# Moving VectorE's row statistics of the feed-forward norm behind the next softmax maxima, in a gated recurrence beside a six-layer local-attention transformer on one core

## Chip, cores and metric

The kernel runs on one core of a Trainium2 chip. The metric is the device time of one execution in microseconds (us), taken from several executions; lower is better. Beside it stands one execution taken with the hardware profiler, whose trace gives the start and length of every instruction on each engine: TensorE (PE), VectorE (DVE), ScalarE (ACT), GpSimd (POOL) and the queue of SyncE (SP), which issues the DMAs.

## The reference, cut to what matters

The input is 2 streams of 1024 tokens of 128 features, in float32. Its normalised form goes through a gated linear recurrence (s) and, independently, through six transformer layers (g); the output is x + s * silu(g).

```python
def attn_layer(x, Wqkv, qs, ksc, Wo):
    q, k, v = jnp.split(x @ Wqkv, 3, -1)          # 16 heads of 64
    q = l2norm(q) * qs; k = l2norm(k) * ksc        # then rotary tables with a decay
    out = local_attention(q, k, v)                 # windows of 32, looking back one window
    return out @ Wo

def ffn_layer(x, g, bln, W1, b1, W2, b2):
    mu = x.mean(-1, keepdims=True)
    var = ((x - mu) ** 2).mean(-1, keepdims=True)
    xn = (x - mu) / jnp.sqrt(var + 1e-05) * g + bln
    a, gate = jnp.split(xn @ W1 + b1, 2, -1)
    return a * jax.nn.gelu(gate, approximate=False) @ W2 + b2

for i in range(DEPTH):                             # DEPTH = 6
    x = attn_layer(shift_tokens(x), ...) + x
    x = ffn_layer(shift_tokens(x), ...) + x
```

## The kernel before

The tokens are cut into 8 tiles of 128, so that six layers make 48 steps. A step i works on one tile of both streams, b = 0 and b = 1, in two half steps, and it is a software pipeline: while the projections of step i run, the keys and queries of step i - 1 are transposed and scored, the softmax and the values of step i - 2 are done, and the feed-forward norm of step i - 3 and the feed-forward of step i - 4 go with the first half step. A step inside its layer is called by its tile, t = 0 to 7. In the last steps (from step 40) the recurrence's work is added.

Every engine has its own instruction stream, written out by hand as a function half(i, b), and the engines wait for each other by semaphores alone. What stands in one half step of an engine is carried out in exactly the written order; a wait holds all that is behind it. There is no scheduler.

What the change and the prediction touch:

- **VectorE.** maxima (line 1561 of the profile, rmax<-ps_s) reads the scores in PSUM when TensorE has filled them (scores_filled). less_max (L1569) subtracts the maxima. rotate (L1535 and L1538, two instructions for each of four chunks of 512 columns) waits for ScalarE's square of the chunk and frees its PSUM bank for TensorE. square_sums is L1548, the gate products of the feed-forward are L1661. mid_variance is the step that moves: two row statistics (L1598), two aggregates (L1601), the negated mean (L1616) and the variance with its epsilon (L1617, ss<-mid_mv), whose semaphore is mid_var.
- **GpSimd.** floor(i, 0) (L1986, floored<-ss) takes the 32 square sums of stream 0 together with the 2 variances of the norm in one instruction of 34 columns, so it waits for both. Behind it stand the Newton step (L1994 to L2000), the scaling of stream 0's keys and queries (L2028), the adds of the rotary halves (L2016), the scaling of probabilities (L2038, pr), the low parts of the projection input (L2051), and then floor(i, 1) for stream 1.
- **ScalarE.** inverse_root (L1208 logarithm, L1212 exponential) waits for the floor. Behind it on ScalarE stand the square of the first chunk (L1166) and the copies of transposed probabilities (L1154, pbd<-ps_tr, two instructions for each of two banks). In half step (i, 1) the first pair of copies stands ahead of the root; in half step (i + 1, 0) both pairs stand behind it, except at a layer's first tile.
- **TensorE.** The transposes of the probabilities (L803) and of the keys (first eight L816 of a half step) share two PSUM banks: the fifth key transpose writes the bank that the second pair of copies (L1154) empties.

Of the kernel before, what the change touches and what calls it, by code (L numbers as in the profile page):

```python
# [91 lines left out]
def valid(step):  # L92

    return not step.fixed or 0 <= step.n < STEPS
# [52 lines left out]
def next_tile(i, b):  # L147
    return (i + 1, 0) if b else (i, 1)
# [215 lines left out]
def layers(nc, a, x, xmid, branch, ident, eps_col, w, rec):  # L364

    with ExitStack() as ctx:
# [152 lines left out]
        def wait_fill(eng, sems, order, i, what):  # L519
            if exists(order, i, what):  # L520
                bank, n = fill(order, i, what)
                eng.wait_ge(sems[bank], n)
# [5 lines left out]
        def softmax_tile(i, b):  # L528
            return (i - 1, 0) if b else (i - 2, 1)
# [21 lines left out]
        with nc.Block() as block:  # L551
# [965 lines left out]
            def _(dve):  # L1517
                v = nc.vector

                def rotate(i, b, c):  # L1520
                    if not valid(i):
                        return
                    k, part = c // 2, slice(c * COLS, (c + 1) * COLS)
                    bank, n = fill(qn_order, i, ("qkv", b, c))
                    if c % 2 == 0:
                        if b:
                            dve.wait_ge(added[0], 2 * i.n + k + 1)
                        elif not i.first:
                            dve.wait_ge(added[1], 2 * i.n + k - 1)
                    if c == 0:  # L1530
                        dve.wait_ge(tab_ready, i.n + 1)
                        after_first(dve, qk_ready[b], 2 * i.n, i)
                    dve.wait_ge(squared[b], 4 * i.n + c + 1)
                    swapped = ps_qn[bank][:, :].rearrange("p (h s d) -> p h s d", s=2, d=DH // 2)[:, :, ::-1, :]
                    v.tensor_tensor(t2[:, part].rearrange("p (h s d) -> p h s d", s=2, d=DH // 2), swapped,  # L1535
                                    tab[:, 2 * k + 1:2 * k + 2, :].rearrange("p o (s d) -> p o s d", s=2)
                                    .broadcast_to([P, HEADS // 2, 2, DH // 2]), ALU.mult)
                    v.tensor_tensor(qk[b][:, part].rearrange("p (h d) -> p h d", d=DH),  # L1538
                                    ps_qn[bank][:, :].rearrange("p (h d) -> p h d", d=DH),
                                    tab[:, 2 * k:2 * k + 1, :].broadcast_to([P, HEADS // 2, DH]),  # L1540
                                    ALU.mult).then_inc(qn_done[bank], 1)
# [15 lines left out]
                def maxima(j, b):  # L1557
                    if not valid(j):
                        return
                    dve.wait_ge(s_full, 2 * j.n + b + 1)  # L1560
                    v.tensor_reduce(rmax[b][:, :], ps_s[:, :, :, :].rearrange("p h m k -> p (h m) k"), AX.X,  # L1561
                                    ALU.max).then_inc(max_ready[b], 1)

                def less_max(j, b):
                    if not valid(j):
                        return
                    dve.wait_ge(max_ready[b], j.n + 1)
                    wait_fill(dve, tr_full, tr_order, j + 1, ("probs", b, 1))
                    v.tensor_tensor(pr[b][:, :, :, :].rearrange("p m h k -> p h m k"), ps_s[:, :, :, :],  # L1569
                                    rmax[b][:, :].rearrange("p (h m) -> p h m", h=2).unsqueeze(3).broadcast_to([P, 2, HP, 2 * WINDOW]),  # L1570
                                    ALU.subtract).then_inc(s_read, 1)
# [21 lines left out]
                def mid_statistics(n):  # L1593

                    dve.wait_ge(fx_in, (n.n + 1) * SHIFT_DMAS)
                    after_first(dve, normed, n.n, n)
                    for s in range(B):
                        v.bn_stats(mid_stats[:, s, :], mid(n, s, MIXED)).then_inc(mid_stat, 1)  # L1598
                    dve.wait_ge(mid_stat, 2 * B * n.n + B)
                    for s in range(B):  # L1600
                        v.bn_aggr(mid_mv[:, s, :], mid_stats[:, s, :]).then_inc(mid_stat, 1)  # L1601
                    dve.wait_ge(mid_stat, 2 * B * (n.n + 1))
# [6 lines left out]
                def mid_variance(i):  # L1609
                    n = i - 3  # L1610
                    if not valid(n):
                        return
                    mid_statistics(n)
                    if not n.first:
                        dve.wait_ge(newton[0], NEWTON * i.n)
                    v.tensor_scalar(minus_mean[:, :], mid_mv[:, :, 0], -1.0, None, ALU.mult)  # L1616
                    v.tensor_scalar(ss[0][:, 2 * HEADS:], mid_mv[:, :, 1], LN_EPS, None, ALU.add).then_inc(mid_var, 1)  # L1617

                def take_out(i, b):
                    if not exists(pv_order, i, ("out", b)):  # L1620
                        return
                    j, m = i - 2 - b, i - 4
                    bank = taken(i, ("out", b))
                    if valid(j):
                        last = residual(bank, j, b)
                    if b == 0 and i.n < STEPS and valid(m):
                        last = update_x(bank, m)
                    last.then_inc(pv_done[bank], 1)
# [100 lines left out]
                def input_stats(columns, part):  # L1729
                    for c in columns:  # L1730
                        dve.wait_ge(x_in[part], 32)
                        v.bn_stats(stats[:, c, :], in_tile(c)).then_inc(s_st, 1)
# [81 lines left out]
                def half(i, b):  # L1814
                    soft = softmax_tile(i, b)
                    maxima(*soft)
                    less_max(*soft)
                    for c in range(4):
                        rotate(i, b, c)
                        if b == 0 and c == 0:  # L1820
                            take_out(i, 1)
                        if (i.n, b, c) == (0, 0, 1):
                            input_stats(range(HEAD, 8), 1)
                        if (i.n, b, c) == (0, 1, 1):
                            input_moments(range(HEAD, COLUMNS), HEAD + COLUMNS)
                        if (i.n, b, c) == (1, 1, 1):
                            copy_pair(0)
                        if c == 1:
                            if b == 1:
                                if i.t == TILES - 1 and not i.last_layer:  # L1830
                                    high_q(i.layer + 1)
                                take_out(i, 0)
                            row_sums(*soft)
                            row_recips(*soft)
                    if b == 0:
                        rec_driving(i - 1, 1)
                    if i.first and b == 0:
                        low_x(i, 1)
                        copy_head(B, HEAD)
                    if (i.n, b) == (1, 1):  # L1840
                        copy_pair(1)
                    if (i.n, b) == (3, 1):
                        softplus_recip()
                    if (i.n, b) == (0, 1):
                        low_x(*next_tile(i, b))
                    rec_conv1d(i, b)
                    recurrent = b == 0 and rec_tile(i, b, RATES_AT) is not None
                    if b == 0 and not recurrent:
                        ffn_gate(i, 0)
                    square_sums(i, b)  # L1850
                    rec_admission(i, b)
                    rec_scan(i, b)
                    if recurrent:
                        ffn_gate(i, 0)
                    if (i.n, b) == (1, 0):
                        low_x(*next_tile(i, b))
                    if b == 0:
                        ffn_gate(i, 1)
                        ffn_gate(i, 2)
                        mid_variance(i)  # L1860
                    elif i.t == 3:
                        low_w1(i.layer)
                    if (i.n, b) == (0, 0):
                        input_stats(range(8, COLUMNS), 1)
                    if (i.n, b) == (0, 1):
                        tables(i + 1)
                        input_root(1)
                    if (i.n, b) == (1, 1):
                        copy_pair(2)
# [407 lines left out]
```

## Time and profile before

| | |
|---|---|
| time, median of 3 runs | 1550.27 us (1549.19 to 1552.37) |
| time of the profiled execution | 1548.62 us |
| its span from first to last instruction | 1546.8 us |
| granted TensorE clock, mean | 0.995 |
| TensorE busy | 1499.9 us, 97% of the span |
| ScalarE busy | 1346.7 us, 87% |
| GpSimd busy | 1291.4 us, 83% |
| VectorE busy | 1283.4 us, 83% |

A busy share is a mean over the span. The profile's times are of one execution; a wait is idle time of the engine ahead of an instruction, with what ended it behind the arrow.

### The profile page before, as it was taken

What the parts mean: (1) busy time and instruction counts of PE and PEld (TensorE: products, weight loads), DVE (VectorE), ACT (ScalarE), POOL (GpSimd) and SP (SyncE); (2) the same over time, 40 slices, a digit from 0 to 9 for tenths busy, and PEclk for the clock granted to TensorE, in tenths of its full rate; (3) what the DMA queues carried; (4) which work ended last, traced back from release to release, by engine and by line L of the source; (5) the groups of instructions that cost most, each with busy time, mean ns of one, the idle gap of its engine ahead of it and who ended that gap; (6) DMA issues with size and microseconds to landing.
All of it is one profiled execution on the core that took longest, in us unless ns stands there. A gap on an engine that the chain in (4) does not pass through costs nothing.

```text
span 1546.8 us, 64269 instructions
## 1 busy us (share of the span) xinstructions
PE 1499.9 (97%) x26170; PEld 1306.7 (84%) x26170; DVE 1283.4 (83%) x2033; ACT 1346.7 (87%) x2600; POOL 1291.4 (83%) x1268
## 2 busy tenths in 40 slices
PE   6899999999999999999999999999999999999996
PEld 3688888888888888888888888888888888888885
DVE  7888888888889878788878878887888878888876
ACT  5779998999998889898989999889899889989974
POOL 8899899978889888899888899888989977767741
PEclk8999999999999999999999999999999999999999
DMA  5344433454343444434354433444433333333232
GB/s 142 88 111 118 100 83 89 103 128 109 87 103 73 101 118 123 96 86 102 74 128 117 102 90 88 101 101 124 108 89 89 86 76 96 91 80 74 65 91 57
DMA packets 219395, 150.44 MB, mean 97 GB/s; under 512 B 144604, under 2 KB 166752, under 8 KB 219104
## 3 DMA queue, kind: packets, MB, share of 16 engines
q1 hardware_dynamic: 219104, 146.33, 39.2%
q8 instruction: 211, 3.46, 1.0%
q14 instruction: 80, 0.66, 0.1%
HBM read 27.50 MB, written 1.05 MB: 18 GB/s over the span
## 4 chain that ended last, share of the span: by engine, by line
PE 81%; issue 5%; POOL 5%; DVE 4%; ACT 4%; SPq 1%; DMA 0%; POOLq 0%; ACTq 0%; DVEq 0%
PE ps_pv L877 11%; PE ps_tr L816 10%; PE ps_pv L909 9%; PE ps_qn L791 8%; PE ps_s L856 8%; PE ps_qn L793 7%; PE ps_qn L792 7%; PE ps_tr L803 5%; PE ps_pv L889 3%; PE ps_s L838 2%; PE ps_pv L927 2%; POOL qk L2016 2%; PE ps_pv L929 2%; PE ps_pv L928 2%; POOL qkr L2028 1%
## 5 line engine op out<-in xcount | busy, mean ns | idle before, releaser
L2016 POOL TENSOR_TENSOR qk<-qk,t 128x1024 f32<-128x1024 f32 x192 | 459.8, 2395 | 1.6 <-ACT v_new L1249 1.1
L2028 POOL TENSOR_TENSOR qkr<-qk,rinv 128x1024 f32<-128x1024 f32 x192 | 363.9, 1907 | 3.7 <-POOL rinv L2000 0.2
L1535 DVE TENSOR_TENSOR t<-ps_qn,tab 128x512 f32<-128x512 f32 x384 | 260.8, 679 | 87.3 <-ACT sq L1166 79.0
L791 PE MATMUL ps_qn<-w_hi,xs_hi 128*128 128x512 f32 x576 | 252.8, 439 | 16.0 <-DVE qk L1538 12.1
L1538 DVE TENSOR_TENSOR qk<-ps_qn,tab 128x512 f32<-128x512 f32 x384 | 261.2, 680 | 0.0
L1166 ACT ACTIVATE sq<-ps_qn 128x512 f32<-128x512 f32 x384 | 229.6, 599 | 27.7 <-PE ps_qn L793 17.9
L1154 ACT ACTIVATE pbd<-ps_tr 64x512 f32<-64x512 f32 x384 | 225.7, 588 | 12.2 <-PE ps_tr L803 8.8
L793 PE MATMUL ps_qn<-w_hi,xs_lo 128*128 128x512 f32 x576 | 229.1, 398 | 0.0
L792 PE MATMUL ps_qn<-w_lo,xs_hi 128*128 128x512 f32 x576 | 228.9, 397 | 0.0
L1548 DVE TENSOR_REDUCE ss<-sq 128x32 f32<-128x2048 f32 x96 | 218.4, 2275 | 0.0
L816 PE MATMUL ps_tr<-ident,qkr 128*128 128x128 f32 x1536 | 210.6, 274 | 5.8 <-ACT pbd L1154 2.5
L877 PEld LDWEIGHTS ps_pv<-pbd,v_win 128*64 128x64 f32 x6144 | 187.5, 138 | 25.2 <-issue 24.7
L816 PEld LDWEIGHTS ps_tr<-ident,qkr 128*128 128x128 f32 x1536 | 175.2, 141 | 34.0 <-issue 18.2
L877 PE MATMUL ps_pv<-pbd,v_win 128*64 128x64 f32 x6144 | 200.9, 224 | 0.0
L2038 POOL TENSOR_TENSOR pr<-pr,rrec 128x1024 f32<-128x1024 f32 x96 | 183.4, 1911 | 16.3 <-issue 11.1
L909 PE MATMUL ps_pv<-wo,oT 128*128 128x128 f32 x1536 | 187.2, 275 | 1.4 <-DVE oT L1555 1.4
L909 PEld LDWEIGHTS ps_pv<-wo,oT 128*128 128x128 f32 x1536 | 182.6, 192 | 6.0 <-DVE oT L1555 1.2
L1561 DVE TENSOR_REDUCE rmax<-ps_s 128x16 f32<-128x1024 f32 x96 | 117.1, 1220 | 67.0 <-PE ps_s L856 64.4
L856 PE MATMUL ps_s<-kT,qT 64*32 64x64 f32 x12288 | 151.7, 225 | 5.2 <-issue 4.8
L856 PEld LDWEIGHTS ps_s<-kT,qT 64*32 64x32 f32 x12288 | 135.1, 105 | 23.5 <-issue 22.3
L791 PEld LDWEIGHTS ps_qn<-w_hi,xs_hi 128*128 128x128 f32 x576 | 109.4, 190 | 46.7 <-issue 16.8
L1986 POOL TENSOR_SCALAR floored<-ss 128x34 f32<-128x34 f32 (+1 forms) x96 | 30.1, 313 | 121.3 <-DVE ss L1617 108.2
(178 smaller groups left out, 3024.8 us busy)
## 6 DMA issues: line engine op xcount, KB each, us to landing
v_win<-v_new SPq DMA_DIRECT2D x576, 128.0 KB
v_win<-v_new SPq DMA_DIRECT2D x192, 64.0 KB
v_win<-v_win SPq DMA_DIRECT2D x188, 64.0 KB, 2.0
kT<-kT SPq DMA_DIRECT2D x84, 128.0 KB, 2.7
w_raw<-in_Wqkv SPq DMA_DIRECT2D x18, 512.0 KB, 3.9
rot<-in_rot SPq DMA_DIRECT2D x48, 128.0 KB, 3.5
wo<-in_Wo SPq DMA_DIRECT2D x6, 512.0 KB, 4.7
x<-x SPq DMA_DIRECT2D x48, 56.0 KB
```

The costliest lines, as they stand in the source:

```text
L791: mm(ps_qn[bank][:, :], xs_hi[b][:, :], w_hi[:, part], start=True, stop=False)
L792: mm(ps_qn[bank][:, :], xs_hi[b][:, :], w_lo[:, part], start=False, stop=False)
L793: mm(ps_qn[bank][:, :], xs_lo[b][:, :], w_hi[:, part], start=False, stop=True).then_inc(qn_full[bank], 1)
L816: last = tr(ps_tr[bank][:, m * P:(m + 1) * P], qkr[b][:, (4 * f + m) * P:(4 * f + m + 1) * P], ident[:, :])
L856: last = mm(ps_s[q, h, hp, :], qT[rows, hp, q], kT[b][rows, hp, WINDOW * w:WINDOW * (w + 2)], start=False, stop=hp == HP - 1)
L877: last = mm(pv_target(bank, hp, w), v_win[b][:, w, hp * DH:(hp + 1) * DH], pbd[:, hp, :, WINDOW * w:WINDOW * (w + 1)], start=True, stop=True)
L909: last = mm(ps_pv[bank][:, 0:P], oT[:, n // 2, n % 2, :], wo[:, n, :], start=(n == 0), stop=(n == HP - 1))
L1166: f(sq[:, c * COLS:(c + 1) * COLS], ps_qn[bank][:, :], ACT.Square).then_inc(squared[b], 1)
L1535: v.tensor_tensor(t2[:, part].rearrange("p (h s d) -> p h s d", s=2, d=DH // 2), swapped, tab[:, 2 * k + 1:2 * k + 2, :].rearrange("p o (s ...
L1538: v.tensor_tensor(qk[b][:, part].rearrange("p (h d) -> p h d", d=DH), ps_qn[bank][:, :].rearrange("p (h d) -> p h d", d=DH), tab[:, 2 * k: ...
L2016: g.tensor_tensor(qk[b][:, part], qk[b][:, part], t2[:, part], ALU.add).then_inc(added[b], 1)
L2028: g.tensor_tensor(qkr[b][:, part].rearrange("p (h d) -> p h d", d=DH), qk[b][:, part].rearrange("p (h d) -> p h d", d=DH), rinv[b][:, k * ...
```

## The change

mid_variance is taken from the end of VectorE's half step (i, 0) and put into half step (i, 1), between maxima and less_max. Nothing else is edited; the instructions and their number stay the same on all engines.

```diff
@@ -1814,6 +1814,8 @@
                 def half(i, b):
                     soft = softmax_tile(i, b)
                     maxima(*soft)
+                    if b == 1:
+                        mid_variance(i)
                     less_max(*soft)
                     for c in range(4):
                         rotate(i, b, c)
@@ -1857,7 +1859,6 @@
                     if b == 0:
                         ffn_gate(i, 1)
                         ffn_gate(i, 2)
-                        mid_variance(i)
                     elif i.t == 3:
                         low_w1(i.layer)
```

VectorE's stream before, around the border between half step (4, 0) and half step (4, 1); the names in square brackets are the semaphores that an instruction waits for:

```order
L1661 SCALAR_TENSOR_TENSOR hid<-ps_pv,b,hid 128x256 [waits gelu_ready]
L1661 SCALAR_TENSOR_TENSOR hid<-ps_pv,b,hid 85x256 [waits gelu_ready]
L1598 BN_STATS mid_stats<-xmid 128x6 [waits mid_normalised,mid_shifted]
L1598 BN_STATS mid_stats<-xmid 128x6
L1601 BN_AGGR mid_mv<-mid_stats 128x2 [waits mid_stats_done]
L1601 BN_AGGR mid_mv<-mid_stats 128x2
L1616 TENSOR_SCALAR minus_mean<-mid_mv 128x2 [waits newton0,mid_stats_done]
L1617 TENSOR_SCALAR ss<-mid_mv 128x2
L1561 TENSOR_REDUCE rmax<-ps_s 128x16 [waits scores_filled]
L1569 TENSOR_TENSOR pr<-ps_s,rmax 128x2x8x64 [waits tr_filled0,max_ready0]
L1535 TENSOR_TENSOR t<-ps_qn,tab 128x512 [waits qk_ready1,squared1,tab_ready,added0]
```

The same place of the changed kernel:

```order
L1661 SCALAR_TENSOR_TENSOR hid<-ps_pv,b,hid 128x256 [waits gelu_ready]
L1661 SCALAR_TENSOR_TENSOR hid<-ps_pv,b,hid 85x256 [waits gelu_ready]
L1561 TENSOR_REDUCE rmax<-ps_s 128x16 [waits scores_filled]
L1598 BN_STATS mid_stats<-xmid 128x6 [waits mid_normalised,mid_shifted]
L1598 BN_STATS mid_stats<-xmid 128x6
L1601 BN_AGGR mid_mv<-mid_stats 128x2 [waits mid_stats_done]
L1601 BN_AGGR mid_mv<-mid_stats 128x2
L1616 TENSOR_SCALAR minus_mean<-mid_mv 128x2 [waits newton0,mid_stats_done]
L1617 TENSOR_SCALAR ss<-mid_mv 128x2
L1569 TENSOR_TENSOR pr<-ps_s,rmax 128x2x8x64 [waits tr_filled0,max_ready0]
L1535 TENSOR_TENSOR t<-ps_qn,tab 128x512 [waits qk_ready1,squared1,tab_ready,added0]
```

The reduction rmax<-ps_s, with its wait for scores_filled, moved ahead of the six instructions of mid_variance; the subtraction behind them stayed where it was. This is so in all 45 steps that have a mid_variance in half().

GpSimd's stream is the same in both kernels. This is what stands behind the wait for mid_var_done there, in half step (i, 1) of a step inside a layer:

```order
L1986 TENSOR_SCALAR floored<-ss 128x34 [waits mid_var_done,ss_sum0]
L1994 TENSOR_TENSOR newt<-rinv 128x34 [waits rooted0]
L1996 TENSOR_TENSOR newt<-newt,floored 128x34 [waits newton0]
L1998 TENSOR_SCALAR newt<-newt 128x34 [waits newton0]
L2000 TENSOR_TENSOR rinv<-rinv,newt 128x34 [waits newton0]
L2008 TENSOR_TENSOR mid_offset<-minus_mean,rinv 128x2 [waits mid_normalised,newton0]
L2028 TENSOR_TENSOR qkr<-qk,rinv 128x1024 [waits tr_filled1,tr_filled0,added0,newton0]
L2028 TENSOR_TENSOR qkr<-qk,rinv 128x1024 [waits tr_filled1,tr_filled0,added0]
L2016 TENSOR_TENSOR qk<-qk,t 128x1024 [waits qn_evacuated1,qn_evacuated0]
L2038 TENSOR_TENSOR pr<-pr,rrec 128x1024 [waits rec_ready0]
L2051 TENSOR_TENSOR xs_lo<-xsh,xs_hi 128x128 [waits tr_evacuated0]
L2016 TENSOR_TENSOR qk<-qk,t 128x1024 [waits qn_evacuated1,qn_evacuated0]
```

Nothing moved here. The next row of this stream is floor(i, 1), which feeds ScalarE's root of stream 1.

## Rows read from the trace of the kernel before

**Rows 1.** The page: the chain that ended last, by engine.
```profile
PE 81%; issue 5%; POOL 5%; DVE 4%; ACT 4%; SPq 1%; DMA 0%; POOLq 0%; ACTq 0%; DVEq 0%
```

**Rows 2.** Busy times in one inner step: PE, PEld, DVE, ACT, POOL, then clock and DMA.
```profile
851.78:881.68 29.90, 29.84 (x540) 26.34 (x539) 24.61 (x40) 26.88 (x52) 25.55 (x25) 1.00 0.44 110
```

**Rows 3.** The waits: engine and line, what it waited for, total us, times, longest.
```profile
POOL floored L1986 <- DVE ss L1617: 108.2, 45, 5.4
```

**Rows 4.** Timeline of VectorE, that step: start us, length us, instruction.
```profile
852.10 0.47 DVE L1598 BATCH_NORM_STATS2 mid_stats<-xmid 128x6 f32<-128x128 f32 x2
...
852.97 0.16 DVE L1617 TENSOR_SCALAR ss<-mid_mv 128x2 f32<-128x2 f32 x1
853.04 1.22 DVE L1561 TENSOR_REDUCE rmax<-ps_s 128x16 f32<-128x1024 f32 x1
854.29 1.23 DVE L1569 TENSOR_TENSOR pr<-ps_s,rmax 128x1024 f32<-128x1024 f32 x1
855.43 0.68 DVE L1535 TENSOR_TENSOR t<-ps_qn,tab 128x512 f32<-128x512 f32 x1
```

**Rows 5.** Timeline of GpSimd, that step.
```profile
853.29 0.29 POOL L1986 TENSOR_SCALAR floored<-ss 128x34 f32<-128x34 f32 x1 [2.10 <-DVE ss L1617]
...
866.70 0.29 POOL L1986 TENSOR_SCALAR floored<-ss 128x32 f32<-128x32 f32 x1
...
883.23 0.29 POOL L1986 TENSOR_SCALAR floored<-ss 128x34 f32<-128x34 f32 x1 [2.84 <-DVE ss L1617]
```

**Rows 6.** Timeline of ScalarE, that step.
```profile
853.80 0.23 ACT L1208 ACTIVATE log_ss<-floored 128x34 f32<-128x34 f32 x1
...
854.33 0.60 ACT L1166 ACTIVATE sq<-ps_qn 128x512 f32<-128x512 f32 x1
...
867.02 0.23 ACT L1208 ACTIVATE log_ss<-floored 128x32 f32<-128x32 f32 x1 [0.66 <-POOL floored L1986]
...
869.12 1.19 ACT L1154 ACTIVATE pbd<-ps_tr 64x512 f32<-64x512 f32 x2
```

**Rows 7.** Timeline of TensorE, that step.
```profile
850.77 1.01 PE L856 MATMUL ps_s<-kT,qT 64*32 64x64 f32 x69
...
858.73 0.40 PE L791 MATMUL ps_qn<-w_hi,xs_hi 128*128 128x512 f32 x1
...
870.62 1.04 PE L816 MATMUL ps_tr<-ident,qkr 128*128 128x128 f32 x8
```

**Rows 8.** Timeline of ScalarE, then TensorE, in step 41.
```profile
1269.46 1.18 ACT L1154 ACTIVATE pbd<-ps_tr 64x512 f32<-64x512 f32 x2
...
1270.79 0.63 PE L816 MATMUL ps_tr<-ident,qkr 128*128 128x128 f32 x4 [0.15 <-ACT pbd L1154]
```

**Rows 9.** Timeline of ScalarE, then TensorE: first and last of 26 steps.
```profile
175.99 1.18 ACT L1154 ACTIVATE pbd<-ps_tr 64x512 f32<-64x512 f32 x2
...
177.31 1.04 PE L816 MATMUL ps_tr<-ident,qkr 128*128 128x128 f32 x8
...
1170.73 1.18 ACT L1154 ACTIVATE pbd<-ps_tr 64x512 f32<-64x512 f32 x2
...
1172.25 1.04 PE L816 MATMUL ps_tr<-ident,qkr 128*128 128x128 f32 x8
```

**Rows 10.** Timeline of GpSimd, then TensorE, at a layer's first tile.
```profile
729.48 1.93 POOL L2038 TENSOR_TENSOR pr<-pr,rrec 128x1024 f32<-128x1024 f32 x1
...
731.76 2.40 POOL L2016 TENSOR_TENSOR qk<-qk,t 128x1024 f32<-128x1024 f32 x1
...
731.46 1.09 PE L803 MATMUL ps_tr<-ident,pr 128*128 128x128 f32 x8 [0.39 <-POOL pr L2038]
```

**Rows 11.** VectorE's negated mean: at that tile, then the group of all 45.
```profile
732.24 1.95 DVE L1616 TENSOR_SCALAR minus_mean<-mid_mv 128x2 f32<-128x2 f32 x1
...
L1616 DVE TENSOR_SCALAR minus_mean<-mid_mv 128x2 f32<-128x2 f32 x45 | 16.3, 363 | 1.5
```

**Rows 12.** Timeline of GpSimd in step 41, one of the recurrence's steps.
```profile
1266.81 0.53 POOL L1986 TENSOR_SCALAR floored<-ss 128x32 f32<-128x32 f32 x1 [1.73 <-DVE ss L1548]
```

## The prediction

> **What bounds the kernel now.** I first read the chain that ended last: TensorE carries 81% of it, and no other engine more than 5% [rows 1]. Then one inner step by its busy times: TensorE is busy 29.84 of 29.90 us at full clock, ScalarE 26.88, GpSimd 25.55, VectorE 24.61 [rows 2]. So inside a layer a step takes as long as TensorE's own work. A delay elsewhere costs time only where it makes TensorE wait, and work saved elsewhere gives nothing. The question is how much slack lies between the moved instructions and TensorE.
>
> Third, the waits. The longest in the kernel is GpSimd's floor waiting for the last instruction of mid_variance: 108.2 us over 45 steps, 2.4 us each [rows 3]. GpSimd has nothing else to do then, so the step that moves is the one that another engine is standing still for. The wait itself costs nothing on TensorE's chain, but it says that whatever delays mid_variance delays everything behind the floor on GpSimd, at once and in full.
>
> Fourth, the timelines of that step. mid_variance starts at 852.10 and ends at 853.13; maxima follow without a gap at 853.04 and take 1.22 us, then less_max at 854.29, then the first rotate at 855.43 [rows 4]. TensorE's scores, which maxima wait for, were complete at 851.78 [rows 7], 0.3 us before mid_variance started. Maxima could therefore have run at 852.10.
>
> **What the change does in such a step.** No instruction is added; the order of two blocks is swapped.
>
> Maxima start at 852.10 instead of 853.04. mid_variance starts behind them at about 853.24 (consecutive VectorE instructions overlap by 0.08) and ends near 854.26, which is 1.13 us later. less_max comes at about the same time as before (it saves the 0.04 us gap ahead of it and gains an overlap, together 0.1 us), so ScalarE's exponentials gain nothing of use.
>
> The floor goes from 853.29 to 854.42, plus 1.13. ScalarE's logarithm started at 853.80, 0.22 us after the end of the floor at 853.58 [rows 5, 6]: ScalarE was still copying. Where it has to wait, it starts 0.03 us behind a floor (867.02 behind 866.99 [rows 5, 6]). So 0.18 us are absorbed and ScalarE's root is 0.95 us late. Queued behind it on ScalarE: the square of the first chunk, the second pair of probability copies, the next square, the exponentials, the key copies. Queued behind its result on GpSimd: Newton, both scalings, add, scaling of probabilities, low_x, add, floor(i, 1).
>
> *First rotate.* Its square ended at 854.93 and will end at 855.88 [rows 6], so rotate starts near 856.0 instead of 855.43. Two chunks later, at about 858.5, it frees the bank that TensorE fills at 858.73 [rows 7]. It just fits: zero, and up to 0.1 us if I am off.
>
> *GpSimd.* From floor(i, 0) to floor(i, 1) pass 13.41 us of work without an idle gap, apart from the wait for the root; floor(i, 1) has no wait of its own in this step [rows 5]. So floor(i, 1) is 0.95 us late too, ending at 867.94 instead of 866.99. ScalarE had already been idle for 0.66 us for it [rows 6], so nothing is absorbed: logarithm, copies, square and copies all come 0.95 late, and the second pair of copies, which ended at 870.31, ends at 871.26.
>
> *TensorE.* The fifth key transpose needs that pair's bank. Eight transposes take 1.04 us and four 0.63, so it starts 0.41 behind 870.62 [rows 7, 8], at 871.03: 0.7 us behind the copies. The least such distance, where TensorE really waits, is 0.15 [rows 8]. Free slack is about 0.57 us and the delay 0.95, so TensorE stalls for 0.38 us. The stall recurs each step, because TensorE, and with it the next scores and the next mid_variance, moves by only 0.38 while GpSimd's lateness begins anew. GpSimd's next floor waited 2.84 us [rows 5], so the delay does not pile up.
>
> I read the same distance in the 26 steps with t = 1 to 6 (steps 5 and 6, and six of each of four layers). The first gives 0.55 us and the last 0.75 by the same rows [rows 9]; the mean is 0.71, the least 0.50, the largest 1.04. Less 0.15, that is 0.56 of slack: **26 x 0.39 = 10 us**.
>
> *Steps 3 and 4.* There the distance was already at its least, 0.14. Their delay, 0.85 and 0.95 us, is paid in full: **1.8 us**.
>
> *Layer borders* (five, from t = 7 to the next layer's t = 0). GpSimd also splits the next layer's weights there and is idle nowhere between the t = 7 floor and the probabilities that TensorE waits for: they end at 731.41, and the transposes start at 731.46 after 0.39 us of idle time [rows 10]. A root that is 0.95 late at t = 7 comes out there whole in four borders, and 0.73 in one where 0.27 us lay between: **4.5 us**.
>
> *The floor at t = 0* doesn't move. There the negated mean took 1.95 us instead of the usual 0.17, and ended (734.19) when GpSimd's add did, at 734.16 [rows 10, 11]. Over the 45 steps this group holds 16.3 us where 45 x 0.17 = 7.7 would do, so 8.7 us of such holding [rows 11]. Moved 1.1 us later it is held until the same moment, so GpSimd's floor comes when it came; but maxima are then done before the hold, and rotate can start up to 0.56 us earlier. GpSimd still limits the next copies, so I give this back **-0.7 us** over the layer starts. Here the Trainium skill has a rule (SBUF — State Buffer, "SBUF: two separate sides"): VectorE and GpSimd share a port pair that is locked for a whole instruction, and the loser blocks completely. By that rule the hold ends with the add, as the trace shows.
>
> *Steps 41 to 47.* The scores come late there, and mid_variance is 2 us later, but floor(i, 1) waits 1.73 us for VectorE's square sums anyway [rows 12]. What is left is a bank or two at 0.1 us: **0.7 us**.
>
> Sum: 10 + 1.8 + 4.5 - 0.7 + 0.7 = 16.3 us. On the profiled execution's 1548.6 us that is 1565; the median of the runs is 1.7 us above it, so I predict **1566 us**, 1.1% slower.
>
> *Bounds of the unknown.* The trace has no floor at the new place. Two numbers carry the sum. The lateness of the root: at most the whole 1.13 us (nothing absorbed), which adds 0.18 to about 33 places, +6 us; at least 0.75, if maxima and the statistics overlap more than neighbours do now, -6 us. The slack: if TensorE can go on at 0.05 behind a release, as in [rows 10], instead of 0.15, -3 us. I stay with 0.95 and 0.15, since rows of the very same instructions show them. A gain on the sum would need TensorE's few waits to vanish, and the change shortens those only at layer starts.
>
> **Rivals.**
>
> *Hidden* (0.09). The 0.95 us are absorbed before TensorE. For it: mid_variance has 2.4 us of GpSimd idle time around it. Against: that idle time lies ahead of the floor, where it protects the next step and not this one, and the distances above are single readings. It needs the root to be less than about 0.55 us late. Result 1549 to 1553.
>
> *Faster* (0.07). The 8.7 us of holding shrink by 1.1 us in each of five places, maxima and less_max come earlier at t = 0, and TensorE's waits for rotate's banks there (0.3 to 0.6 us each) go. Worth up to 2 or 3 us if the root's lateness is free; it decides only from there. Against: TensorE's layer starts are limited by GpSimd. By the port rule of the Trainium skill, named above, a later negated mean is held for less, which is this case. Result about 1547.
>
> *Nothing absorbed* (0.14). The lateness passes to TensorE whole, 0.95 us in each of 38 steps, because rotate's bank and the copies miss one after the other: 36 us, 1586.
>
> *Queue position.* That ScalarE's late key and value copies cost TensorE a second time in half step (i, 1), about 0.22 us, is not a case of its own: TensorE arrives later at the fifth key transpose by as much, and waits less there.
>
> **Chances.** Forecast 0.70. For 1566 alone, 1558 to 1574. The range of eight in ten reaches down to a mostly hidden delay and up past the forecast's own upper bound: 1555 to 1577. A median within 0.2%, 3.1 us, of 1550.3 counts as no change, about what a measurement can tell: 0.09. Faster 0.07, slower 0.84.
>
> **What the changed profile would show.** Right: the wait of the floor for L1617 grows by about 0.6 us per inner step (1.13 later, on a step 0.38 longer, with GpSimd arriving 0.95 later); the floor starts about 2.3 us after the end of VectorE's gate product instead of 1.2; the logarithm of 34 columns has an idle gap of nearly 1 us with the floor as its releaser, in nearly all 45 steps, where it now has one in five; TensorE's wait for pbd copies at L816, now rare, appears in most inner steps with 0.2 to 0.7 us; inner steps take 30.2 to 30.4 us; the negated mean's group falls from 16.3 to about 10 us, with no gain on the floor at t = 0. Wrong: inner steps still at 29.9 us, or TensorE waiting first for VectorE's banks (L791). The prediction fails if copies and transposes have more room than their present distance shows.

## The result and the profile after

| | before | after |
|---|---|---|
| median, us | 1549.73 (1548.05 to 1552.37, 4 runs) | 1573.32 (1573.01 to 1573.8, 4 runs) |
| profiled execution, us | 1548.62 | 1573.8 |
| its span, us | 1546.8 | 1572.0 |

The ratio is 1.015, with a 95% interval of 1.0138 to 1.0163: 23.6 us slower by the medians. The forecast was 1566 with 1555 to 1577, so the sign and the way were right and the size was a third too small: 16.3 us forecast, 23.6 measured.

The page of the changed kernel, the chain that ended last by engine (answers to [rows 1], where TensorE had 81%):

```profile
PE 47%; DVE 14%; POOL 12%; issue 11%; ACT 10%; SPq 4%; DMA 1%; POOLq 0%; ACTq 0%; DVEq 0%
```

TensorE has the same work, but the chain now leaves it again and again for waits on the other engines.

The waits of the changed kernel: engine and line, what it waited for, total us, times, longest (the lines of GpSimd are one higher after the edit, so L1987 is the floor).

```profile
POOL floored L1987 <- DVE ss L1617: 148.4, 45, 7.2
DVE t L1535 <- ACT sq L1166: 128.3, 178, 2.6
ACT log_ss L1208 <- POOL floored L1987: 85.4, 83, 2.4
...
PEld ps_qn L791 <- DVE qk L1538: 27.7, 58, 1.0
...
PE ps_tr L816 <- ACT pbd L1154: 5.9, 12, 1.1
...
PE ps_pv L877 <- DVE x L1591: 2.5, 5, 0.5
```

For comparison, the same waits of the kernel before that are not among its rows above:

```profile
DVE t L1535 <- ACT sq L1166: 79.0, 93, 1.6
ACT log_ss L1208 <- POOL floored L1986: 29.9, 31, 2.0
PEld ps_qn L791 <- DVE qk L1538: 11.1, 20, 0.8
PE ps_tr L816 <- ACT pbd L1154: 2.5, 5, 1.1
```

The floor's wait grew from 108.2 [rows 3] to 148.4 us, 0.9 us for each of the 45 (0.6 was forecast for an inner step). The logarithm waits for the floor 83 times instead of 31, rotate for a square 178 times instead of 93. On TensorE the new waits are not mainly where the forecast had them: at the fifth key transpose (L816) there are 12 instead of 5, but at L791, the projection that needs a PSUM bank which rotate (L1538) empties, there are 58 instead of 20, 38 more (PEld is TensorE's weight load).

One inner step of the changed kernel in busy times, the same step as in [rows 2], from its first transpose of probabilities (L803, right behind the scores) to that of the next step:

```profile
867.07:897.51 30.44, 30.26 (x545) 26.35 (x539) 24.89 (x40) 26.61 (x52) 25.51 (x25) 1.00 0.41 98
```

It takes 30.44 us; between the same two transposes (851.71 to 881.68) the kernel before takes 29.97, so 0.47 us are lost. The timelines of that step show the forecast's chain and where it went further. First VectorE:

```profile
867.54 1.21 DVE L1561 TENSOR_REDUCE rmax<-ps_s 128x16 f32<-128x1024 f32 x1
868.67 0.47 DVE L1598 BATCH_NORM_STATS2 mid_stats<-xmid 128x6 f32<-128x128 f32 x2
...
869.53 0.16 DVE L1617 TENSOR_SCALAR ss<-mid_mv 128x2 f32<-128x2 f32 x1
869.60 1.22 DVE L1569 TENSOR_TENSOR pr<-ps_s,rmax 128x1024 f32<-128x1024 f32 x1
869.85 0.29 POOL L1987 TENSOR_SCALAR floored<-ss 128x34 f32<-128x34 f32 x1 [3.39 <-DVE ss L1617]
...
870.17 0.23 ACT L1208 ACTIVATE log_ss<-floored 128x34 f32<-128x34 f32 x1 [0.97 <-POOL floored L1987]
```

Maxima stand first, the statistics behind them, and the logarithm has the idle gap of nearly 1 us. The chain that ended last in the same stretch (start, length, what) goes on from there:

```profile
870.70 0.60 ACT sq L1166
...
871.78 0.59 ACT pbd L1154
...
872.39 0.61 ACT sq L1166
...
873.02 0.69 DVE t L1535
873.72 0.61 DVE qk L1538
...
874.37 0.50 PE ps_qn L791
```

The square that counts is the *second* one, at 872.39. It stands behind the root, the first square and the two copies (the second of them is shown), and the second rotate waits for it. TensorE's projections at that place, timeline of the changed kernel:

```profile
873.31 0.48 PE L791 MATMUL ps_qn<-w_hi,xs_hi 128*128 128x512 f32 x1
...
873.85 0.40 PE L793 MATMUL ps_qn<-w_hi,xs_lo 128*128 128x512 f32 x1
874.37 0.50 PE L791 MATMUL ps_qn<-w_hi,xs_hi 128*128 128x512 f32 x1
```

The last row comes 0.52 behind the product ahead of it, where two products of one bank start 0.23 apart (873.62 and 873.85). These 0.29 us are lost at rotate's bank; the two L791 are 1.06 us apart instead of 0.78. Another 0.09 goes right behind: the product after the late one starts 0.34 behind it (874.71), not 0.23. The next values (L877) start 2.74 us behind the key transposes instead of 2.36 (872.51 to 875.25, 857.16 to 859.52), so 0.38 us are lost in all. I call this gate 1, and the copies ahead of the fifth key transpose gate 2. Gate 2 is reached later in the same step:

```profile
885.43 1.18 ACT L1154 ACTIVATE pbd<-ps_tr 64x512 f32<-64x512 f32 x2
...
886.32 1.07 PE L816 MATMUL ps_tr<-ident,qkr 128*128 128x128 f32 x8
```

The fifth transpose starts 0.41 + 0.03 behind 886.32 (the group of eight took 0.03 more than 1.04), so at 886.76, and the copies end at 886.61: the distance is at its least, 0.15, but TensorE lost only about 0.03 there, since gate 1 had delayed it already. What is left of the 0.47, nearly 0.1 us, falls within the next scores, which take 1.70 us instead of 1.61, and no wait explains it.

### The profile page after: what moved, and what is told of

Same layout as the page of the kernel before. It is cut to its first block, busy times and chain, and to the rows that moved or that the text cites. A ratio compares the mean times of both kernels' runs of the same rounds, so it can differ in the third digit from the quotient of the medians.

```text
span 1572.0 us, 64269 instructions
## 1 busy us (share of the span) xinstructions
PE 1513.6 (96%) x26170; PEld 1305.9 (83%) x26170; DVE 1276.7 (81%) x2033; ACT 1333.6 (85%) x2600; POOL 1289.0 (82%) x1268
## 4 chain that ended last, share of the span: by engine, by line
PE 47%; DVE 14%; POOL 12%; issue 11%; ACT 10%; SPq 4%; DMA 1%; POOLq 0%; ACTq 0%; DVEq 0%
PE ps_pv L877 8%; PE ps_tr L816 6%; PE ps_qn L791 5%; PE ps_pv L909 5%; PE ps_s L856 5%; DVE ss L1548 4%; POOL qk L2017 4%; PE ps_qn L793 4%; PE ps_qn L792 4%; POOL qkr L2029 3%; PE ps_tr L803 3%; ACT pbd L1154 3%; ACT sq L1166 3%; DVE rmax L1561 2%; DVE t L1535 1%
## 5 line engine op out<-in xcount | busy, mean ns | idle before, releaser
L791 PE MATMUL ps_qn<-w_hi,xs_hi 128*128 128x512 f32 x576 | 256.2, 445 | 19.4 <-DVE qk L1538 12.6
L1538 DVE TENSOR_TENSOR qk<-ps_qn,tab 128x512 f32<-128x512 f32 x384 | 261.3, 681 | 0.0
L816 PE MATMUL ps_tr<-ident,qkr 128*128 128x128 f32 x1536 | 214.4, 275 | 9.1 <-ACT pbd L1154 5.9
L877 PEld LDWEIGHTS ps_pv<-pbd,v_win 128*64 128x64 f32 x6144 | 189.3, 139 | 28.1 <-issue 27.8
L816 PEld LDWEIGHTS ps_tr<-ident,qkr 128*128 128x128 f32 x1536 | 175.4, 141 | 40.8 <-issue 24.3
L877 PE MATMUL ps_pv<-pbd,v_win 128*64 128x64 f32 x6144 | 202.9, 225 | 2.5 <-DVE x L1591 2.5
L1987 POOL TENSOR_SCALAR floored<-ss 128x34 f32<-128x34 f32 (+1 forms) x96 | 31.9, 332 | 157.1 <-DVE ss L1617 148.4
L791 PEld LDWEIGHTS ps_qn<-w_hi,xs_hi 128*128 128x128 f32 x576 | 109.4, 190 | 61.0 <-DVE qk L1538 27.7
```

Of the source, the lines that this page charges most:

```text
L791: mm(ps_qn[bank][:, :], xs_hi[b][:, :], w_hi[:, part], start=True, stop=False)
L816: last = tr(ps_tr[bank][:, m * P:(m + 1) * P], qkr[b][:, (4 * f + m) * P:(4 * f + m + 1) * P], ident[:, :])
L877: last = mm(pv_target(bank, hp, w), v_win[b][:, w, hp * DH:(hp + 1) * DH], pbd[:, hp, :, WINDOW * w:WINDOW * (w + 1)], start=True, stop=True)
```

## Experiments

All times are medians, ratios go by runs of the kernel before on the same chip.

**1 and 2. The floor without the variances.** The floor and the root take only the 32 square sums, and GpSimd waits for mid_var first where it needs the negated mean. Left out is the variance's part: the norm's factor is a constant 0 (its memset is not shown) instead of the inverse root of the variance. Once with the old place of mid_variance, once with the new.

```diff
         def root_span(s, b, n):
-            return 0 if valid(s) else 2 * HEADS, 2 * HEADS + B if b == 0 and valid(n) else 2 * HEADS
+            return 0 if valid(s) else 2 * HEADS, 2 * HEADS
...
                     pool.wait_ge(newton[0], NEWTON * (i.n + 1))
+                    pool.wait_ge(mid_var, n.n + 1)
```

> The old order, but the floor, root and Newton step of stream 0 no longer take the two norm variances; the norm's rows are multiplied by a constant 0 instead of by their inverse deviation, so the variance's part is left out of the result. GpSimd waits for mid_variance only at the norm's offset, behind the Newton step. Theory A (all the loss of the changed kernel passes through the floor's wait for mid_variance): about as the kernel before, 1547 to 1551, because in inner steps the root was already held by ScalarE's copies (0.22 us), not by the floor. Theory B (the loss comes from VectorE's own order, less_max and rotate): the same here, this run is the reference for the next.

> The new place of mid_variance with the same freed floor and the same part left out. Theory A: within 2 us of the run with the old place, that is near 1549, since nobody on the way to the root waits for mid_variance. Theory B: still about 20 us slower than the run with the old place, near 1570. A mix of the two lies between in proportion.

Old place: 1547.63 us, ratio 0.9996 (0.9985 to 1.0006). New place: 1545.69 us, ratio 0.9977 (0.9964 to 0.999). The waits of the second kernel:

```profile
DVE t L1535 <- ACT sq L1166: 80.1, 91, 1.6
POOL floored L1987 <- DVE ss L1548: 26.6, 31, 1.8
ACT log_ss L1208 <- POOL floored L1987: 25.5, 31, 2.0
...
PEld ps_qn L791 <- DVE qk L1538: 9.9, 19, 0.8
```

There is no wait for L1617 any more, and with it every other wait is back at the level of before. With the same instructions on VectorE in the same new order, nothing is lost; the medians even differ by 1.9 us the other way, though the intervals of the two ratios overlap a little. So the whole 23.6 us pass through the floor's wait, and VectorE's own order costs nothing. The rival theory that the order on VectorE itself costs time falls.

**3, 4, 9 and 10. The new place in part of the steps.** A condition chooses the place step by step; only its line differs.

```diff
+                def late_place(i):
+                    return 9 <= i.n < 40 and 1 <= i.t <= 6      # inner steps
+                    # i.n >= 41 (the recurrence's steps)
+                    # 7 <= i.n < 41 and i.t in (7, 0) (borders)
+                    # i.n <= 6 (first steps)
...
+                    if b == 1 and late_place(i):
+                        mid_variance(i)
...
-                        mid_variance(i)
+                        if not late_place(i):
+                            mid_variance(i)
```

> mid_variance at the new place only in the 24 inner steps (t = 1 to 6) of the four layers from step 9 to 38; the old place elsewhere. Theory A with the prediction's sizes: 24 x 0.39 = 9.4 us, 1559. If the inner steps are where the sum was too small, 13 or more (1563); if the shortfall is at the ends and borders, 9 to 11.

> mid_variance at the new place only in steps 41 to 47, those with the recurrence. Prediction's size: plus 0.7 us, 1550.4. The profile of the changed kernel has these steps 3.6 us longer, of which 2.4 are two gaps of 1.2 us in the scores that end without any releaser: if they belong to the change, plus 3 to 4 us; if they are fetches that fall where they like, plus 1.

> mid_variance at the new place only in the steps with t = 7 and t = 0 from step 7 to 40 (five borders). Prediction's sizes: 4.5 us from GpSimd's lateness less 0.7 us at the layer starts, plus 4, so 1553. The profile of the changed kernel adds a wait of 0.5 to 0.6 us at L877 at three borders, for VectorE's L1591 behind the weight rounding of t = 7: with it the sum per border stays near 1 us, so the total is 4 to 6 us; above 8 something else acts there.

> mid_variance at the new place only in steps 3 to 6. Prediction's sizes: 1.8 us for steps 3 and 4 and 0.9 for steps 5 and 6, 2.7 us, 1552. If the two-gate loss of rotate's bank and the full lateness apply from the start: 4 us, 1553.5.

| steps with the new place | forecast | median, before | difference | ratio (95%) |
|---|---|---|---|---|
| 24 inner steps | +9.4 | 1561.03, 1549.43 | +11.6 | 1.0075 (1.0057 to 1.0093) |
| steps from 41 on | +0.7 | 1554.62, 1549.43 | +5.2 | 1.0027 (1.0014 to 1.004) |
| t = 7 and t = 0 | +3.8 | 1553.41, 1550.43 | +3.0 | 1.003 (1.0016 to 1.0044) |
| steps up to 6 | +2.6 | 1552.35, 1550.43 | +1.9 | 1.0013 (0.9999 to 1.0027) |

The forecasts are the prediction's own terms (24 x 0.39; 4.5 - 0.7; 1.8 and 2 x 0.39). The difference is between the two medians; by the ratios the four parts are 11.6, 4.2, 4.6 and 2.0 us. The ratios less one add to 0.0145, 22.5 us, beside 0.0150 for the whole change. So the parts add up, and by either count the largest error stands in the recurrence's steps, the only ones whose forecast lies outside the interval.

**5, 6, 7 and 8. The two gates one by one.** ScalarE's order is changed so that the late root no longer holds what a gate waits for. *Square first*: in half steps b = 1 the first square stands ahead of the root, which frees gate 1. *Copies first*: in half steps b = 0 the first pair of copies stands ahead of the root, as it already does at a layer's first tile, which frees gate 2. The first three kernels have the new place of mid_variance, the last has the old one.

```diff
-                    root_first = b == 0 and (i.t > 0 or i.first)
+                    root_first = i.first and b == 0               # copies first
...
-                    if not root_first and not i.first:
+                    if not root_first and not i.first and b == 0: # square first
                         inverse_root(*norm_tile(i, b), i - 3)
                     square(i, b, 0)
+                    if not i.first and b == 1:                    # square first
+                        inverse_root(*norm_tile(i, b), i - 3)
                     evac_probs(i, b, 1)
```

> The changed kernel, with ScalarE's square of stream 1's first chunk put ahead of the root of stream 0 in half step (i, 1). The late root then no longer delays rotate and the bank that TensorE waits for (theory of two gates: about 0.3 us per inner step is now paid at L791 in half step (i, 1), and the late copies of half step (i + 1, 0) would take 0.4 if the first were gone). Two gates: little comes back, 0 to 4 us, 1569 to 1573, and the wait moves to L816. If the VectorE bank alone were the cause: 8 to 12 us come back, near 1562.

> The changed kernel, with the first pair of probability copies put ahead of the root in half step (i + 1, 0), so that ScalarE works while it waits for the floor. The copies behind the root then come about 1.1 us earlier than in the changed kernel. The prediction's single cause (late copies hold the fifth key transpose): most of the inner steps' loss goes, 10 us or more, 1563 or less. Two gates: the bank of rotate still costs 0.3 us per inner step, so 4 to 7 us come back, mostly where that gate is not in front (t = 3), 1566 to 1569.

> Both edits of ScalarE's order on the changed kernel. Two gates: the inner steps lose nothing any more; what is left is GpSimd's lateness at the layer borders (about 4 us) and some of the ends, so 1552 to 1557. If a third cause in the inner steps exists: above 1560.

> Both edits of ScalarE's order on the kernel before. Inner steps had no such stall, so nothing there; ScalarE idles less for the floor at layer starts and in steps 3 and 4. 1545 to 1551; if putting the root later delays GpSimd's Newton step more than it helps, 1552 to 1560.

| kernel | median | ratio (95%) | L791 waits for L1538 or L1540 | L816 waits for pbd |
|---|---|---|---|---|
| changed kernel | 1573.32 | 1.015 (1.0138 to 1.0163) | 58 times, 27.7 us | 12, 5.9 |
| square first | 1572.42 | 1.0146 (1.0131 to 1.0161) | 10, 6.0 | 26, 13.9 |
| copies first | 1567.88 | 1.0116 (1.0101 to 1.0131) | 58, 29.4 | 3, 2.2 |
| both | 1556.22 | 1.0043 (1.0028 to 1.0059) | 10, 6.0 | 2, 2.5 |
| both, old place | 1555.17 | 1.0041 (1.0026 to 1.0056) | 15, 7.9 | 2, 2.6 |

Freeing gate 1 alone brings 0.9 us, which the intervals do not tell from nothing, gate 2 alone 5.4, both together 17.1. Each gate stands ready behind the other. TensorE's timeline with the square first shows it in an inner step:

```profile
873.35 0.48 PE L791 MATMUL ps_qn<-w_hi,xs_hi 128*128 128x512 f32 x1
...
874.12 0.40 PE L791 MATMUL ps_qn<-w_hi,xs_hi 128*128 128x512 f32 x1
...
885.87 0.60 PE L816 MATMUL ps_tr<-ident,qkr 128*128 128x128 f32 x4
886.79 0.63 PE L816 MATMUL ps_tr<-ident,qkr 128*128 128x128 f32 x4 [0.32 <-ACT pbd L1154]
```

The two L791 are 0.77 apart again, and the transposes are now split by a wait of 0.32 us: the loss has moved from gate 1 to gate 2. With the copies first it is the other way round, the transposes in one piece and the bank late, with 1.04 us between the two L791:

```profile
865.70 0.48 PE L791 MATMUL ps_qn<-w_hi,xs_hi 128*128 128x512 f32 x1
...
866.74 0.50 PE L791 MATMUL ps_qn<-w_hi,xs_hi 128*128 128x512 f32 x1
...
878.64 1.04 PE L816 MATMUL ps_tr<-ident,qkr 128*128 128x128 f32 x8
```

With both, neither is seen; the two L791 are 0.78 apart and the eight transposes in one piece:

```profile
858.87 0.48 PE L791 MATMUL ps_qn<-w_hi,xs_hi 128*128 128x512 f32 x1
...
859.65 0.40 PE L791 MATMUL ps_qn<-w_hi,xs_hi 128*128 128x512 f32 x1
...
871.41 1.04 PE L816 MATMUL ps_tr<-ident,qkr 128*128 128x128 f32 x8
```

With both orders the new place costs no more than the old one (1.0043 and 1.0041). The two orders cost the kernel before about 6 us themselves, where 1545 to 1551 was expected, so they are no way to make it faster; in the one profile of each, VectorE's maxima of the steps from 40 on lie 5 to 7 us further apart than before, and those of the inner steps do not. The cause stays open.

**11 and 12. An earlier place.** If the floor's 108 us of waiting were worth something, mid_variance ahead of one or of two of the gate products should be faster.

```diff
                         ffn_gate(i, 1)
-                        ffn_gate(i, 2)
                         mid_variance(i)
+                        ffn_gate(i, 2)
```

> The other direction: mid_variance ahead of the last gate product in the old half step, so 0.4 us earlier in inner steps, and inside VectorE's 1.4 us wait for that product in the steps with the recurrence. Late-root theory: ScalarE's copies hold the root 0.2 us already, so inner steps gain nothing; layer starts and the last steps may gain a little: 1546 to 1550. If an earlier floor were worth as much as a later one costs: 1540.

> mid_variance one product earlier still, 0.9 us ahead of the old place. At layer starts the negated mean then runs before GpSimd's add begins and is held by nothing (it took 1.8 to 2.15 us there), so maxima and rotate come up to 1.8 us earlier in five steps: late-root theory gives 1545 to 1550. Against: both products and the bank that TensorE needs for the down projection come 1 us later; if that has no slack, 1555 or more.

1550.6 us, ratio 1.0002 (0.9991 to 1.0013), and 1552.32 us, ratio 1.0009 (0.9997 to 1.0021): no difference that can be measured. The delay costs, and its opposite gives nothing. That agrees with TensorE being the bound at the old place, and with the 0.22 us for which the logarithm had stood behind ScalarE's copies [rows 5, 6]. None of the ten kernels that leave no work out is faster than the kernel before.

## Why the prediction was right, and where its size was off

**The way.** It was forecast that the moved step delays the floor by 1.13 us, ScalarE's root by 0.95 and TensorE through what stands behind the root. The logarithm's gap of 0.97 us in the timeline, the floor's wait and the pair of kernels with a free floor show each link. *Hidden*, *Faster* and *Nothing absorbed* fall: an inner step costs 0.47 us in the timeline and 0.48 by the kernel with the 24 inner steps (11.6 / 24), neither 0 nor 0.95.

**The step that failed** is "First rotate ... Two chunks later, at about 858.5, it frees the bank that TensorE fills at 858.73. It just fits: zero". The start of the first rotate was right: 0.57 us late was forecast; measured from the first key transpose, it came 0.64 late (871.42 - 872.51 against 855.43 - 857.16 in the kernel before). But the second rotate does not follow the first back to back. It waits for the second square, which before ended at 856.63, while the first chunk's second instruction was still busy, and in the changed kernel ends at 872.99, behind a root, a square and two copies that are all late. So nothing of the lateness is absorbed for the second chunk: its rotate ends at 874.33, which counted from the first key transpose is 858.98 in the times of the kernel before, not 858.5, and the bank is 0.29 us late for TensorE. I had followed the first instruction of a group and taken the others to come with it.

These two rows of the kernel before, ScalarE's second square and VectorE's second rotate in the step of [rows 4 to 7], are the ones that I should have used:

```profile
856.03 0.60 ACT L1166 ACTIVATE sq<-ps_qn 128x512 f32<-128x512 f32 x1
...
856.66 0.69 DVE L1535 TENSOR_TENSOR t<-ps_qn,tab 128x512 f32<-128x512 f32 x1
```

The rotate starts 0.03 us behind the square even there: no slack at all.

**Why the term came out almost right all the same.** The forecast for an inner step, 0.39 us, was made at gate 2. In series the step loses what the tighter one asks, not the sum: 0.38 at gate 1 and about 0.03 at gate 2. The sign that was forecast for it, a wait of 0.2 to 0.7 us at L816 in most inner steps, did not appear, and what was named as a sign of being wrong, TensorE waiting first for VectorE's banks, did. So the total lay within its range for a reason that was half wrong, and that two different gates ask nearly the same is luck.

**The steps with t = 3.** Between maxima of stream 1 the inner steps lie about 0.34 us further apart on average, but the two steps around t = 3 together 1.2, 1.2, 1.3 and 1.6 in the four layers instead of 0.7. The first pair, before and after (timeline of VectorE: 325.46 to 385.50, 60.04 us, and 332.70 to 393.94, 61.24 us):

```profile
325.46 1.23 DVE L1561 TENSOR_REDUCE rmax<-ps_s 128x16 f32<-128x1024 f32 x1 [2.02 <-PE ps_s L856]
...
385.50 1.23 DVE L1561 TENSOR_REDUCE rmax<-ps_s 128x16 f32<-128x1024 f32 x1 [2.43 <-PE ps_s L856]
```

```profile
332.70 1.23 DVE L1561 TENSOR_REDUCE rmax<-ps_s 128x16 f32<-128x1024 f32 x1 [1.45 <-PE ps_s L856]
...
363.53 0.87 DVE L1672 TENSOR_TENSOR w_lo<-w,w_hi 128x682 fp32r<-128x682 f32 x1 [2.02 <-ACT w_hi L1228]
363.75 0.80 POOL L1987 TENSOR_SCALAR floored<-ss 128x32 f32<-128x32 f32 x1
...
393.94 1.22 DVE L1561 TENSOR_REDUCE rmax<-ps_s 128x16 f32<-128x1024 f32 x1 [1.67 <-PE ps_s L856]
```

There VectorE splits weights (L1672) once per layer. Before, the floor of stream 1 came first, at 355.45, and took its 0.29; L1672 followed at 355.82. Now the floor comes second and takes 0.80, until just after L1672 is done (364.40). The 0.5 us are added to the lateness of the root, and TensorE pays them at gate 2. Before, L1672 held the Newton step behind the floor instead (L1994, 0.87 us for 0.24), for which the copies do not wait. I had looked for such holding only in the other direction. Over four layers that is about 2.5 us and as much as the inner steps exceeded their term by (11.6 against 9.4; the 9.4 itself still lies within that kernel's interval, 8.8 to 14.4). Copies first shrinks the four pairs to 0.4, 0.4, 0.7 and 0.7, as it should if gate 2 is where they are paid.

**Layer borders and first steps.** 3.8 and 2.6 us were forecast, 3.0 and 1.9 measured, both within their intervals of some 2 us either way. The holding at t = 0 shrank as forecast (what time that gave back was not measured apart): the negated mean's group fell from 16.3 us [rows 11] to

```profile
L1616 DVE TENSOR_SCALAR minus_mean<-mid_mv 128x2 f32<-128x2 f32 x45 | 9.5, 211 | 1.6
```

What was not seen there is a second bank: VectorE's rounding of the next layer's weights (L1668, 2.05 us) stands ahead of the add that empties a bank of the values. In the kernel before it started at 466.30 and the add ended 1.02 us behind the start of the values (L877, 467.87), in time; now it starts behind the late second rotate, the add ends 1.54 us behind that start (477.71), and TensorE waits, in five places 2.5 us together; the kernel with the new place at the borders alone has the same five. Timeline of the changed kernel:

```profile
476.68 2.05 DVE L1668 CAST w_hi<-w_raw 128x512 fp32r<-128x512 f32 x1
...
478.84 0.41 DVE L1591 TENSOR_TENSOR x<-ps_pv,xmid 128x256 f32<-128x256 f32 x1
...
479.40 1.15 PE L877 MATMUL ps_pv<-pbd,v_win 128*64 128x64 f32 x32 [0.54 <-DVE x L1591]
```

**The recurrence's steps** were forecast at 0.7 us and cost 5.2 (1.0027, so 2 to 6 us). Here the reason was wrong. It was taken from floor(i, 1), which waits for VectorE's sums anyway; that gate 1 sits behind the *other* floor was the same oversight as above. In the kernel with the new place in those steps alone, TensorE waits for L1538 at L791 26 times and 12.3 us, instead of 20 and 11.1: gate 1 is there in six more places, but worth only 1.2 us. In the changed kernel's profile TensorE also stands still twice for about 1.2 us within a set of scores, ahead of the 102nd matmul of one and the 106th of another, without a releaser. The second:

```profile
1430.95 0.42 PE L856 MATMUL ps_s<-kT,qT 64*32 64x64 f32 x23 [1.18 <-issue]
```

The change is not needed for them. Ahead of the same two matmuls TensorE also stands still in kernels whose steps there have the old place: in the one with the new place at the borders alone, and in the one with the old place and both orders of ScalarE.

```profile
1309.24 0.44 PE L856 MATMUL ps_s<-kT,qT 64*32 64x64 f32 x27 [2.02 <-issue]
```

```profile
1416.43 0.42 PE L856 MATMUL ps_s<-kT,qT 64*32 64x64 f32 x23 [1.68 <-issue]
```

At two more such places (1231.49 and 1491.05, 1.38 and 2.32 us) the kernel before has them too. From 1200 us on, every gap of this kind in all 14 profiles (0.7 us and more) stands ahead of one of the same four matmuls; which of them come and how long they are differs from profile to profile. In the profile of the kernel with the new place from step 41 on, the maxima from there to the last step's lie 2.4 us further apart than before (1220.11 to 1497.30, 1216.69 to 1491.46), and about 0.9 us of these are such gaps (1.48, 1.18 and 1.98, together 4.64, for 1.38 and 2.32, together 3.70). That leaves about 1.5 us, near the 1.2 at gate 1. Why the medians say 4 to 5 us stays open.

**The sum.** Forecast 9.4, 2.6, 3.8 and 0.7; measured 11.6, 1.9, 3.0 and 5.2. The error of 7 us is 4.5 in the recurrence and 2.2 in the inner steps by the medians, 3.5 and 2.2 by the ratios, with 0.8 at the borders. In the inner steps t = 3 accounts for it; in the recurrence it is open.

## What to carry to other kernels

Where a chain of single-buffered hand-offs runs in rounds, follow every instruction behind the late one that some engine waits for, not the first of its group: the second rotate had no slack (0.03 us) where the first had 0.5 us between its square (854.93) and its start (855.43). Two gates in series hide each other, so the trace shows only the one that comes first and taking it away brings next to nothing (0.9 us) while both together bring 17. And a long wait of an idle engine (108 us here) is no reserve: moving its releaser earlier gave nothing, moving it 1.1 us later cost 0.3 to 0.5 us in an inner step.

## What the runs showed of the hardware

A small GpSimd instruction that starts beside a long VectorE one is held for it, 0.80 us instead of 0.29 beside L1672, as a small VectorE instruction is beside GpSimd's add (1.95 instead of 0.17 [rows 11]). In these rows the one that comes second is held, so a shift of 1 us can turn it round. The Trainium skill (SBUF — State Buffer, "SBUF: two separate sides") has one port pair shared by the two engines: between GpSimd and a VectorE instruction in a two-port mode or with two inputs in SBUF, whichever starts first keeps it for the whole instruction. The trace agrees in both directions: the floor ends 0.15 us behind L1672, the negated mean 0.03 behind the add.

The granted clock differs between profiles early on: windows of 60 to 70 us, before and after (PE, PEld, DVE, ACT, POOL busy, clock, DMA share, GB/s).

```profile
60.00:70.00 10.00, 8.68 (x159) 6.63 (x163) 8.35 (x12) 8.73 (x17) 9.90 (x7) 1.00 0.27 66
```

```profile
60.00:70.00 10.00, 8.42 (x92) 6.96 (x92) 6.44 (x11) 8.21 (x16) 8.88 (x7) 0.83 0.13 31
```

The kernel with the new place from step 41 on has the same instructions as the kernel before up to there, and its profile shows 0.83 in this window too. So this belongs to the run and not to the change; it makes the changed kernel's profile about 2 us late before the first moved instruction (transposes of probabilities at 86.69 instead of 84.67 and at 100.66 instead of 98.63). In windows of 1 us the clock there is 0.61, 0.50, 0.50 and 0.69 from 62 to 66 (0.50 is 1.2 of 2.4 GHz), behind one in which TensorE was busy for 0.09 us; in the kernel before it was busy for 0.34 us in that one and the clock stayed at 1.00.
